# A residual stack of 128 conditioned samples: the rest of W0 behind the rest of W2, powers made later, and a new order in the preparation

## What is computed

```
x = x + x @ W0[subject]^T + b0[subject]                      # 8 subjects
x = x + rotation(x, a = amp ** dt[s], angle = freq * dt[s])  # cos, sin per pair of rows
x = x + x @ W2[category] + b2[category]                      # 64 categories
h = relu(x @ W1[language] + b1[language])
z = x + h @ Wup[language] + bup[language]                    # 10 languages
x = (z - mean) / sqrt(var + eps) * gamma[language] + beta[language]
```

## Time and profile before

| | us |
|---|---|
| median of 3 runs | 1139.03 (1137.39 to 1139.06) |
| the profiled execution, its own time | 1133.95 |
| its span, first to last instruction | 1131.2 |
| TensorE matmuls busy | 1105.2 (98%), 6074 records |
| VectorE busy | 919.6 (81%) |
| ScalarE busy | 776.5 (69%) |
| GpSimd busy | 709.6 (63%) |
| DMA | 355.08 MB, mean 314 GB/s |

### The profile page before, as it was taken

The page is one execution under the profiler, slowest core; times in us unless marked ns, Lnnn a source line. Parts: engine busy times, 40 slices in busy tenths (PEclk is TensorE's granted clock), DMA queues, the critical chain, the costliest instruction groups (busy, mean ns, idle before and its releaser), DMA issues.

```text
span 1131.2 us, 28478 instructions
## 1 busy us (share of the span) xinstructions
PE 1105.2 (98%) x6074; PEld 925.7 (82%) x6074; DVE 919.6 (81%) x1355; ACT 776.5 (69%) x1821; POOL 709.6 (63%) x861
## 2 busy tenths in 40 slices
PE   7999999999999999999999999999999999999996
PEld 5778888887788888888788888887888888788885
DVE  7789987878877787788888877778878788888876
ACT  4676767767676676777677667667677677676764
POOL 6689976567655655656656655656565666565563
PEclk9999999999999999999999999999999999999998
DMA  8998979888997998899799889888987999798981
GB/s 293 363 403 314 314 272 353 311 300 310 368 316 276 339 325 304 298 332 346 281 329 367 295 289 346 305 306 325 338 318 276 335 322 350 273 377 299 318 296 74
DMA packets 98135, 355.08 MB, mean 314 GB/s; under 512 B 11936, under 2 KB 12066, under 8 KB 80384
## 3 DMA queue, kind: packets, MB, share of 16 engines
q1 hardware_dynamic: 96624, 352.10, 87.4%
q10 hardware_dynamic: 1296, 0.80, 0.2%
HBM read 318.51 MB, written 34.34 MB: 312 GB/s over the span
## 4 chain that ended last, share of the span: by engine, by line
PE 90%; DMA 3%; DVE 2%; issue 2%; SPq 2%; ACT 1%; DVEq 0%; POOL 0%; POOLq 0%; ACTq 0%
PE ps_mix L1114 10%; PE ps_l L1141 10%; PE ps_l L1103 10%; PE ps_l L1087 9%; PE ps_l L1131 9%; PE ps_l L1135 9%; PE ps_hT L1161 9%; PE ps_l L1098 5%; PE ps_x3T L1151 5%; PE ps_l L1091 5%; PE ps_y L1181 2%; PE ps_y L1184 2%; PE ps_y L1182 2%; DVE w_lo L911 1%; DMA rows<-sample_rows 1%
## 5 line engine op out<-in xcount | busy, mean ns | idle before, releaser
L656 ACT ACTIVATE w_hi<-w_in 128x1024 fp32r<-128x1024 f32 x256 | 270.9, 1059 | 226.8 <-POOL w_in L513 226.8
L911 DVE TENSOR_TENSOR w_lo<-w_in,w_hi 128x1024 fp32r<-128x1024 f32 x256 | 344.1, 1344 | 18.1 <-ACT w_hi L656 16.8
L526 POOL TENSOR_SCALAR var_eps<-square_sum 128x1 f32<-128x1 f32 x128 | 24.4, 190 | 374.7 <-DVE w_lo L911 290.4
L940 DVE TENSOR_TENSOR x<-ps_l,rows 128x512 f32<-128x512 f32 x126 | 87.0, 690 | 114.2 <-PE ps_l L1141 112.7
L702 ACT ACTIVATE x3T<-ps_x3T,minus_bup 128x128 f32<-128x128 f32 x512 | 145.9, 367 | 37.0 <-PE ps_x3T L1151 35.5
L545 POOL TENSOR_TENSOR x_beta<-x,rows 128x512 f32<-128x512 f32 x128 | 168.5, 1316 | 0.0
L513 POOL TENSOR_TENSOR w_in<-w_in,ident 128x512 f32<-128x512 f32 x128 | 165.4, 1292 | 2.0 <-DMA w_in<-W 1.2
L520 POOL TENSOR_TENSOR x_lo<-x_in,x_hi 128x512 fp32r<-128x512 f32 x127 | 163.9, 1291 | 1.0 <-ACT x_hi L632 1.0
L1087 PE MATMUL ps_l<-w_hi,x_hi 128*128 128x512 f32 x512 | 151.2, 417 | 0.0
L1114 PEld LDWEIGHTS ps_mix<-mix,x 128*128 128x128 f32 x1024 | 124.3, 191 | 31.4 <-issue 29.7
L1141 PE MATMUL ps_l<-w_lo,x2T_hi 128*128 128x512 f32 x512 | 139.1, 391 | 6.0 <-DVE w_lo L911 6.0
(11 more groups left out here) (150 smaller groups left out, 1874.2 us busy)
## 6 DMA issues: line engine op xcount, KB each, us to landing
w_in<-W SPq DMA_DIRECT2D x128, 1024.0 KB, 6.4
rows<-sample_rows SPq DMA_DIRECT2D x128, 768.0 KB, 7.0
x_in<-xT SPq DMA_DIRECT2D x128, 256.0 KB, 6.1
w_in<-W SPq DMA_DIRECT2D x128, 256.0 KB, 5.0
out<-yb SPq DMA_DIRECT2D x128, 256.0 KB, 6.6
w_in<-W0T SPq DMA_DIRECT2D x7, 1024.0 KB, 5.1
w_in<-W0T SPq DMA_DIRECT2D x4, 512.0 KB, 5.8
wup_raw<-Wup SPq DMA_DIRECT2D x7, 256.0 KB, 6.1
```

What stands on the lines that cost most here:

```text
L656: act.activation(w2_hi[:, halves[n]], w2_in[s % WB][:, halves[n]], ACT.Copy).then_inc(w2_hi_made, 1)
L911: dve.tensor_tensor(w2_lo[:, half], w2_in[s % WB][:, half], w2_hi[:, half].bitcast(fp32), ALU.subtract).then_inc(w2_lo_made, 1)
```

## The change

It has six parts. On VectorE, rest_of_w0(s+1) moves behind rest_of_w2(s, 1) from turn 2 on (turn 1 keeps its order), and TensorE's l0_back(s) waits, from s = 3 on, for mix_made(s+1) after its two x_lo matmuls. GpSimd makes the groups of powers in turns 9 to 21. The first two samples' coefficients are made by four ScalarE activations, and make_diag(0) comes before round_x(1). There are 18 and 10 idle matmuls, the 10 behind a wait for the second one-hot operand. down(0) stands before rotate(1). In turn 1 ScalarE copies x3T before it rounds x and W2.

```diff
-    COEF_FIRST, COEF_TURN = 24, 8
+    COEF_FIRST, COEF_TURN, COEF_FROM = 24, 8, 9
...
+        ones_col = stats_cols[:, 39:40]
...
-            pool.wait_ge(zeroed, 4)
+            pool.memset(ones_col, 1.0).then_inc(zeroed, 1)
+            pool.wait_ge(zeroed, 5)
...
             fold_early_w0(0, 1)
-            pool.wait_ge(pair_trig_made, 1)
-            pool.tensor_tensor(sin1[:, 0:2], pair_power, pair_trig[:, 0:2], ALU.mult).then_inc(pair_made, 1)
-            pair_link(pool.tensor_tensor(cos1[:, 0:2], pair_power, pair_trig[:, 2:4], ALU.mult))
-            pool.tensor_scalar(cos1[:, 0:2], cos1[:, 0:2], 1.0, None, ALU.add).then_inc(pair_made, 1)
             fold_w2(0)
...
-                if s < len(coef_groups):
-                    powers(coef_groups[s])
-                    coefficients(coef_groups[s], 2 + s)
+                group = s - COEF_FROM + 1
+                if 1 <= group < len(coef_groups):
+                    powers(coef_groups[group])
+                    coefficients(coef_groups[group], 2 + group)
...
             act.activation(pair_trig, pair_red, ACT.Sin).then_inc(pair_trig_made, 1)
+            act.wait_ge(pair_trig_made, 1)
+            for n in range(2):
+                act.activation(cos1[:, n:n + 1], pair_trig[:, 2 + n:3 + n], ACT.Identity, bias=ones_col,
+                               scale=pair_power[:, n:n + 1]).then_inc(pair_made, 1)
+                act.activation(sin1[:, n:n + 1], pair_trig[:, n:n + 1], ACT.Copy,
+                               scale=pair_power[:, n:n + 1]).then_inc(pair_made, 1)
+            act.wait_ge(consts_made, 3)
+            act.wait_ge(pair_made, 4)
+            make_diag(0)
             round_x(1)
-            act.wait_ge(consts_made, 3)
-            act.wait_ge(pair_made, 2)
-            make_diag(0)
...
+                if s == 1:
+                    copy_x3T(s, lang)
                 if s < LAST - 1:
                     round_x(s + 2)
                     round_w0(s + 2, first)
...
-                copy_x3T(s, lang)
+                if s > 1:
+                    copy_x3T(s, lang)
...
-                if s < LAST:
+                if s == 1:
+                    rest_of_w0(s + 1, (0, 1), first)
+                rest_of_w2(s, 1)
+                if 2 <= s < LAST:
+
                     rest_of_w0(s + 1, (1,) if in_two_turns(s + 1) else (0, 1), first)
-                rest_of_w2(s, 1)
...
-            stay_busy(6)
-            stay_busy(12)
+            stay_busy(18)
+            pe.wait_ge(onehot_made, 2)
+            stay_busy(10)
             pe.wait_ge(onehot_made, 4)
...
                     pe.matmul(ps_l0[:, :], x_lo[s % 2][:, c * N:(c + 1) * N], w0_hi[s % 2][:, c * D:(c + 1) * D],
                               start=False, stop=False)
+                if s >= 3:
+                    pe.wait_ge(mix_made, s + 1)
...
             l0_back(1)
+            down(0)
             rotate(1)
-            down(0)
```

More of the change, by code:

```diff
@@ L703, in copy_x3T @@
                                    bias=minus_bup[:, bass.ds(lang + c * L, 1)]).then_inc(x3T_made, 1)
-            act.wait_ge(zeroed, 4)
+            act.wait_ge(zeroed, 5)
             act.activation(idle_col, minus_half[:, :], ACT.Sin)
@@ L880, in make_mix @@
                 if s == 0:
-                    dve.wait_ge(pair_made, 2)
+                    dve.wait_ge(pair_made, 4)
                 dve.wait_ge(diag_made, s + 1)
```

## The result

The changed kernel takes **1128.92 us** (median of 7 runs, 1128.07 to 1130.69), the kernel before 1137.18 beside it (7 runs, 1132.12 to 1139.06): ratio 0.994 [0.9922, 0.9957], faster by 0.6%. The prediction was 1135.8, range 1132.3 to 1139.0. Run twice more among the experiments the changed kernel gave 0.9935 [0.9917, 0.9953] and 0.9939 [0.9926, 0.9952]. So the sum is about -7 where I said -3.2. The sign and the large parts were right, the size was not. Part of the distance between 1135.8 and 1128.92 is the starting point: the median of three runs that I started from, 1139.03, was itself high, as the 99 later runs of the kernel before have a median of 1135.61.

A forecast was written before the change was run, and what follows sets the result against it. TensorE's fixed matmul order bounds the kernel, with gains only where it stands still. Terms -2.3 (w0_lo), -0.8 (powers) and -0.1 (preparation) sum to -3.2 us: 1130.75 profiled, 1135.8 with the runs' 5 us offset; range 1132.3 to 1139.0.

The forecast's parts named there:

- the seven long turns: Turns bringing a new W0: the pair 4.3 us too long, single ones such as 1.36, TensorE waiting for w2_lo's second half.
- Everything TensorE gains before 66 us is lost in that wait: Preparation and turns 1 to 4: earlier TensorE work gains nothing unless the rows of sample 4 land earlier.
- Part 1: w0_lo behind w2_lo in turns with a new W0: saves VectorE's idle time ahead of x1, -2.3 us.
- Part 2: Powers moved to turns 9 to 21: -0.8 us in sum, bounds -1.4 and 0.
- The +0.5 for turns 9 to 21: Eight turns newly carrying powers without Wup cost 0.07 us each, +0.5 in sum.
- Turns 2 to 4 end in the wait for rows, so nothing there: Taking the powers out of turns 2 to 4 gains nothing, as these turns end waiting for rows.
- Parts 3 and 4: Preparation: ScalarE's first diagonal and more idle matmuls let the store of rows be issued 0.9 us earlier (0.4 to 1.4).
- Parts 5 and 6: Orders of turn 1: TensorE's gain nil at turn 4's wait; Wup loaded earlier delays the store 0 to 2.0 us, 0.8 taken.
- (b): Rival: rows land 0.9 us earlier and VectorE has unseen slack at w0_lo; -5.5 us, 1133.5; chance 0.13.
- (a): Rival: rows land 1.1 us later, or idle time in turn 4 halves the clock; -1.8 us, 1137.2; chance 0.20.
- (c): Rival: w0_lo collides with GpSimd's fold in turns with a new W0; -1.0 us, 1138.0; chance 0.10.
- (d): Rival: TensorE's new wait at the first w0_lo matmul costs in all 125 turns; +10 us, 1145.8; chance 0.04.

The follow-up runs named there:

- c_after: The changed kernel run once more as a control, with nothing changed: 1128.48 us.
- the filler: Kernel before plus 3 idle matmuls ahead of the second half of the first w0_lo products and 12 ahead of rotate(0): 1134.16 us, 0.9992.
- b_turn1: Kernel before with down(0) ahead of rotate(1) and x3T copied first in turn 1, powers still early: 1137.5 us, ratio 1.0013.

## Why the prediction was wrong in size

- **What bounds the kernel: one of three points failed.** TensorE's order and the seven long turns were read rightly. "Everything TensorE gains before 66 us is lost in that wait" was not. It rested on one profiled execution, whose span of 1131.2 at a clock of .996 is at the fast end of the kernel's own runs; the second profile of the same kernel has no such wait. The step holds in the traces whose clock did not fall behind 16 us, and in one of the three of the changed kernel (1.73 us in c_after). The 99 executions have a mean clock of .9946, below the profile's .996, so the wait cannot be counted on in most of them. I had noted that the median stood 5 us above the profiled execution, and applied the same difference to both kernels. That difference was the kernel's own variable preparation, and part of the change acts on just that: **-2.4 us** by the split above, -1.2 at the lower price per 0.001. By the first it is the largest miss of the sum. The range of the three runs shown (1137.39 to 1139.06) beside 1133.95 was the sign of it.
- **Part 1, -2.3 taken:** -2.8 to -2.9 measured. The mechanism held: x1 follows VectorE's queue without a gap, regular turns are at 8.43 to 8.45, single turns and the one behind them save 0.34 to 0.40 together. The term was undersized by 0.5 to 0.6.
- **Part 2, -0.8 taken:** -0.9 in the rest by the runs (-0.7 in its own batch), 0.9 to 1.7 us less in turns 5 to 8 by trace, so inside the bounds. The +0.5 for turns 9 to 21 is not seen: from turn 8 to turn 24 after takes 135.44 against 135.83. "Turns 2 to 4 end in the wait for rows, so nothing there" failed, but only together with the orders: there the power costs 1.9 in one place, and late powers spare it.
- **Parts 3 and 4, a store 0.9 earlier:** the diagonal came 1.6 earlier (15.49 against 17.12), but the store landed no earlier. The three traces of the changed kernel issue it at 26.81, 27.26 and 30.41 (27.39 and 28.70 in the two of before) and it lands at 35.1, 36.0 and 35.3 (35.4 and 35.3). The term of -0.9 is thus seen in no run. That the clock's loss would move was right, but I put it to the idle matmuls ahead of the sort; these show nothing (0.9939 without them). The gap ahead of rotate(0), which I had not priced, goes with it. Behind gaps of 1.88 us (the second profile of before) and 2.31 us (GpSimd's diagonal) the clock stood at .58 and .50 from 20 to 24 us. Behind 0.84 it kept 1.00 to 24 us in both repeats of the changed kernel and fell between 24 and 32; in the profile of after it fell at once, behind two gaps of 0.78 and 0.84. The Trainium skill (TensorE: Matmul & The Clock Gate, § A second HAM failure mode: psum-queue depth-cycling) describes another kernel, in which short idle times of TensorE between groups of matmuls, as it goes through the PSUM banks, make the clock fall and rise again. The execution of after may be of that kind, but the case does not settle it: c_after, with gaps of 1.46 and 0.84 in the same two places, kept 1.00 from 16 to 24 us.
- **Parts 5 and 6, nil:** nil in the changed kernel at equal clock, as said, and the trace of that kernel with the old orders does wait for the rows (1.74 us). What I missed is that without late powers they cost 2.1. SyncE's early load of Wup shows no delay of the store, though the prediction took one as likely (0.8). Issued at 30.58, 4.3 us before the store landed (changed kernel with early powers), it left the store at 8.4 us, against 8.2 with Wup issued at 33.03 (the diagonal alone). The rows of sample 4 were issued at 56.70, 56.31 and 55.41 in the three traces of the changed kernel (55.68 and 55.86 before), and in one of the three turn 4 waited for them, 1.73 us.
- **The rivals.** (b), the front survives, came nearest (-5.5), by its idea; its slack in part 1 was there too (0.5 of the 0.9). (a) did not occur: the rows were issued 1.0 later in the profile of after, but nothing waited for them, and the clock stayed at 1.00 behind turn 4. Nor did (c). (d), the new wait in each turn: six waits in all, no regular one.

What stays open: why the stretch at the lower clock differs between executions of one kernel was not tried. That the clock's part is caused by the gap ahead of rotate(0) is argued, not shown. For it: the filler raised the mean clock as much as the diagonal did in the same batch (.9964 and .9962 against .9950). Against: its gain in time (0.9992 [0.9978, 1.0006]) is within what can be told from none. How much time the clock itself gives back is therefore known only from the fit and from the lengths of the stretches.

## What to carry to other kernels

When the median lies some us above the profiled execution and the runs spread, that spread is itself a term: look for the stretch that makes it (here the preparation, by the clock of each run) and ask what the change does to it, instead of carrying the difference over. A wait that hides gains must be seen in more than one execution before gains ahead of it are put at nil. And take out a part as well as add it alone: the two differed here by 3 us for the powers, because another part had spent the slack that they used to hide in.

## What the runs showed of the hardware

- The 99 executions of one kernel differ by up to 7.9 us of span (1130.0 to 1137.9) and their mean clocks by 0.991 to 0.998; at 0.991 the spans are some 6.5 us above those at 0.997 by the fitted line. In the profiles the lower clock stands at 12 to 16 us, or in stretches between 18 and 36 us, or nowhere in the front, and in all of them for the last 4.4 to 7.4 us, behind the last matmul.
- Fillers that keep the clock are not free: 15 idle matmuls raised the mean clock by .0014 over the kernel before of the same batch and cost 0.6 to 0.8 us otherwise; 16 in the changed kernel cost 0.5 to 1.2 with no gain.
- Of a GpSimd addition of 128x512 and a VectorE subtraction of 128x1024 side by side, the later one was slow: begun at 41.94 against 41.95, the addition took 1.27 us and the subtraction 2.34 instead of 1.21 (before); begun at 48.08 against 47.74, the addition took 2.28 and the subtraction 1.47 (b_turn1). A queue in fixed order passed that on to each step behind it.
- The store of the rows (768 KB), issued at 26.4 to 32.7 us in the 18 traces, landed at 34.9 to 37.0: the latest issue, 6.2 us behind the earliest, landed 1.8 us behind it.
